# Decoder of twelve sublayers: row-max placements of the short attentions move to the ScalarE queue, and the wide-head attention becomes one Block

## The chip, the core and the metric

One core of a Trainium2 chip runs the whole kernel in one launch. The metric is the device time in microseconds (us); the kernel before took 1625.39 us in the median of 3 runs (1624.26 to 1627.04). The engines are TensorE (PE; its weight loads are listed as PEld), VectorE (DVE), ScalarE (ACT), GpSimd (POOL) and SyncE (SP). SP computes nothing here: it only waits and issues transfers.

## The reference, cut to what matters

A decoder of four layers, each of self-attention, cross-attention and feed-forward, every one with a norm and a residual. x is 8 x 256 x 128 and ctx 8 x 512 x 128, in f32.

```python
x = x + _L0_attn_ref(_layernorm(x, axis=-1), ...)       # linear attention
x = x + _L0_xattn_ref(_layernorm(x, axis=-1), ctx_1024, ...)   # 16 heads of 8, 512 keys
x = x + _L0_ffn_ref(_layernorm(x, axis=-1), ...)        # experts
x = x + _L1_attn_ref(_layernorm(x, axis=-1), ...)       # attention over the batch
x = x + _L1_xattn_ref(_layernorm(x, axis=-1), ctx_1024, ...)   # ONE head of 128, 512 keys
x = x + _L1_ffn_ref(_layernorm(x, axis=-1), ...)
x = x + _L2_attn_ref(_layernorm(x, axis=-1), ...)
x = x + _L2_xattn_ref(_layernorm(x, axis=-1), ctx_1024, ...)   # 16 heads of 8, 512 keys
x = x + _L2_ffn_ref(_layernorm(x, axis=-1), ...)
x = x + _L3_attn_ref(_layernorm(x, axis=-1), ...)       # 16 heads of 8, 256 keys, causal
x = x + _L3_xattn_ref(_layernorm(x, axis=-1), ctx_1024, ...)   # the same with a key mask
x = x + _L3_ffn_ref(_layernorm(x, axis=-1), ...)
```

Each attention is softmax(q k^T / sqrt(d)) v, with the row maximum taken off before the exponential.

## The kernel before

The stages follow each other in `decoder`. A stage is one `Block`: in it each engine runs a program of its own, ordered against the others by semaphores, and at its end all engines meet. The activations lie transposed in SBUF, features on the partitions: xT (128 x 2048) and its norm xn.

**The narrow attentions** (16 heads of 8) are `narrow_attention` = `project` + `attend_wide` (512 keys, in layers 0 and 2) or `attend_short` (256 keys, causal: layer 3's self-attention, then its cross-attention). `project` makes q and k and splits each into three bf16 parts. SP stores the parts to DRAM scratch with `store_parts` (L744) and reads them back with `load_stacks` (L1004) as stacks: `q_stack[par]` and `k_stack[par]` hold, for a pair of heads, 48 rows of part products, a mask row, and in q_stack two rows for the negated row maximum, split into two bf16 parts. There are two stacks of each, by the parity of the batch, and a stack is loaded in two halves of four head pairs.

The attention runs in steps s = 0 to 8, and step s works on two batches at once: in front, the scores of batch s, from which DVE takes the row maxima (L1544); behind, the logits, exponentials and sums of batch b = s - 1. Step 0 has only a front, step 8 only a back. A step goes through i = 0 to 15, one head each. In `attend_short` PE does for each i: with i even a mask matmul for the scores (L1405), then in `logit_bank` a wait until the exponential of head i - 2 is done (there are two logit banks), then the scores (L1422, L1424) and logits (L1444, L1446) of head i; at odd i a piece of the sums with v (L1459, L1461), which waits until POOL has masked the diagonals (L1132) of the group's four exponentials. ACT does the 16 exponentials of a step (L1521, 128 x 384).

A row maximum reaches the stack in this way, once per half hf of the 16 heads: DVE (L1553), POOL splits it into two parts (L1104, L1106), PE transposes it (`turn_max`, L1155; at i = 11 for half 0 of batch s, at i = 3 of the next step for half 1), ACT copies it to `max_rows` (`keep_max`, L1169), and SP issues two transfers of it into `q_stack` (`place`, L1063). PE waits for that placement, and for the loads of the stack, in `attend_halves` at i = 0 and i = 8.

SP's order is written out in `attend_transfers`. For 256 keys (`early`) it is: both halves of load(1), place(0,0), wait for all parts, store k of batches 2 and 3, place(0,1), store q of batches 2 to 7, and then for each s: load(s,1), place(s-1,1), a k store at s = 2 and 3, load(s+1,0), place(s,0). load(2, .) waits for the whole q store and the first k store (`stored_q`, `stored_k1`), and for the logits that free the stack. Every placement stands behind what SP issued or waited for before it.

**The wide-head attention** (L1_xattn) comes after `batch_attention` and takes three Blocks: `fetch` (SP loads its weights), `layer_norm` (PE, ACT and DVE), and `wide_head_attention`, in which SP then begins to load ctxT (L2300), POOL copies xn (L2310), and PE projects q (L2328), k (L2332) and v (L2337) of a batch and makes the scores (L2356), again with the back of the batch before beside the front of the next. A norm is a chain over four tiles of 512 columns: mean (PE, L230), centring (DVE, L265), squares (ACT), variance (PE, L207), root (ACT), reciprocal (DVE, L271), spread (PE, L207), scaling (DVE, L280).

Of the kernel before, what the change touches and what calls it, by code (L numbers as in the profile page):

```python
# [323 lines left out]
def norm_dve(norm, dve):  # L324
# [7 lines left out]
    for t in range(4):  # L332
        if t < 2:
            norm.invert(dve, t + 2)
        norm.scale(dve, t)


def layer_norm(c, padded=None):

    norm = Norm(c, Carver(c), padded=padded)
    with c.nc.Block() as block:

        @block.tensor
        def _(pe):
            norm_pe(norm, pe)

        @block.scalar  # L350
        def _(act):
            norm_act(norm, act)

        @block.vector
        def _(dve):
            norm_dve(norm, dve)
    norm.advance()


class FirstLoads:  # L360
# [681 lines left out]
    body(B // 2, 0, False, True, True)  # L1042


def attend_transfers(c, buf, sp, nk, key_mask, made):


    g = c.sig

    def load(b, hf):  # L1050

        if b > 1:

            sp.wait_ge(g["logits"].sem, g["logits"].at((b - 2) * H + H // 2 * (hf + 1)))
            sp.wait_ge(g["stored_q"].sem, g["stored_q"].at(STORES))
            sp.wait_ge(g[f"stored_k{b // 2}"].sem, g[f"stored_k{b // 2}"].at(STORES))
        load_stacks(c, sp, b % 2, hf, b * S, b * nk, nk, b * S if key_mask else None)

    def place(s, hf):

        sp.wait_ge(g["turned_out"].sem, g["turned_out"].at(s * 2 + hf + 1))
        for e in range(2):
            sp.dma_start(c.q_stack[s % 2][64 * e + ROW_MAX:64 * e + ROWS, HALF * hf:HALF * hf + HALF, :],  # L1063
                         buf.maxrow[hf][8 * e:8 * e + 8, :]).then_inc(g[f"max_placed{hf}"].sem, 16)

    for hf in range(2):
        load(1, hf)
    early = nk == S
    if early:
        place(0, 0)  # L1070
    sp.wait_ge(g["parts"].sem, g["parts"].at(made.parts))
    if early:
        store_parts(c, sp, "k", nk, 1, 2, g["stored_k1"].sem)
        place(0, 1)
    store_parts(c, sp, "q", nk, 1, B // 2, g["stored_q"].sem)
    if not early:
        store_parts(c, sp, "k", nk, 1, 2, g["stored_k1"].sem)
        place(0, 0)
        place(0, 1)
    for s in range(1, B + 1):  # L1080
        k = s if early else s + 1
        if s > 1:
            if s < B:
                load(s, 1)
            place(s - 1, 1)
        if 2 <= k < 4:
            store_parts(c, sp, "k", nk, k, k + 1, g[f"stored_k{k}"].sem)
        if s < B - 1:
            load(s + 1, 0)
        if s < B:  # L1090
            place(s, 0)
    for hf in range(2):
        sp.wait_ge(g[f"max_placed{hf}"].sem, g[f"max_placed{hf}"].at(32 * B))

# [287 lines left out]
def attend_short(c, key_mask, made, gated=False):  # L1382
# [115 lines left out]
    def scalar(act):  # L1498

        act.activation(c.small[:, 648:649], c.consts[:, C_EPS:C_EPS + 1], ACT.Exp)  # L1500

        def keep(grp, b):
            act.wait_ge(g["summed"].sem, g["summed"].at(b * GROUPS + grp + 1))
            act.activation(buf.summed[:, grp, bass.ds(b * S, S)], ps[:, 6 + grp % 2, 0:S], ACT.Identity)\
               .then_inc(g[f"summed_out{grp % 2}"].sem, 1)

        def step(it, par, front, back, before):
            first = isinstance(it, int) and it == 0
            s = it * 2 + par
            b = s - 1  # L1510
            for i in range(H):
                if back and i == 3:
                    keep_max(c, buf, act, b, 1, first)
                if front and i == 11:
                    keep_max(c, buf, act, s, 0, first and par == 0)
                if back:
                    act.wait_ge(g["logits"].sem, g["logits"].at(b * H + i + 1))

                    if not (first and i < 8):
                        act.wait_ge(g["summed"].sem, g["summed"].at(b * GROUPS + (i - 8) // 4 + 1))  # L1520
                    act.activation(buf.probs[i % 8][:, 0:3 * P], ps[:, 4 + i % 2, 0:3 * P], ACT.Exp, scale=scale)\  # L1521
                       .then_inc(g["probs"].sem, 1)
                if before and i == 4:
                    keep(3, s - 2)
                if back and i == 12:
                    keep(1, b)
            if not front:
                keep(3, b)
        attend_steps(nc, ENG.Activation, step)
# [730 lines left out]
              spread=2 * NU, residual=NU, out_proj=NU, probs=NU, max_raw=NU, summed=2 * NU, recip=NU)  # L2260


def wide_head_attention(c, slot):


    nc, g, ps = c.nc, c.sig, c.ps
# [8 lines left out]
    pr = [cv.f32(2, SC) for _ in range(2)]  # L2275
    pT = cv.f32(nch, S)
    sm = c.small
    mx, nb, sums, rec = (fold(sm[:, 4 * i:4 * i + 4], (2, 2)) for i in range(4))
    SCALE = D ** -0.5

    def steps(engine, body):
# [7 lines left out]
    with nc.Block() as block:  # L2289

        @block.sync
        def _(sp):
            def body(it):
                for par in range(2):
                    b = it * 2 + par
                    at = b * SC if isinstance(it, int) else sp.snap(b * SC)
                    if not isinstance(it, int):

                        wait_counted(c, sp, g["v_proj"].sem, g["v_proj"].at(b - 1))
                    sp.dma_start(csrc[par][:, :], c.io["ctxT"][:, bass.ds(at, SC)]).then_inc(g[f"src_in{par}"].sem, 16)  # L2300
            pairs(nc, ENG.SP, body)

        @block.gpsimd
        def _(pool):
            def body(it):
                for par in range(2):
                    b = it * 2 + par
                    if not isinstance(it, int):
                        pool.wait_ge(g["v_proj"].sem, g["v_proj"].at(b - 1))
                    pool.tensor_copy(qsrc[par][:, :], c.xn[:, bass.ds(b * S, S)]).then_inc(g["staged"].sem, 1)  # L2310
            pairs(nc, ENG.Pool, body)

        @block.tensor
        def _(pe):
            pe.wait_ge(g[f"loaded{slot}"].sem, g[f"loaded{slot}"].at(16))

            def step(it, par, front, back):
                first = isinstance(it, int) and it == 0 and par == 0
                second = isinstance(it, int) and it == 0 and par == 1
# [2 lines left out]
                if front:  # L2322
# [15 lines left out]
                                       w[:, W_V:W_V + P], start=True, stop=True)  # L2338
                    mm.then_inc(g["v_proj"].sem, 1)
                if back:  # L2340
                    for t in range(2):
                        pe.wait_ge(g["normed"].sem, g["normed"].at(b * 2 + t + 1))
                        if not second:
                            pe.wait_ge(g["turned_out"].sem, g["turned_out"].at((b - 1) * 2 + t + 1))
                        for ch in range(nch):
                            mm = pe.transpose(ps[:, 5 + t, ch * P:(ch + 1) * P], pr[prv][:, t, ch * P:(ch + 1) * P],
                                              c.ident[:, :])
                        mm.then_inc(g["turned"].sem, 1)
# [9 lines left out]
                if back:  # L2358
                    pe.wait_ge(g["turned_out"].sem, g["turned_out"].at(s * 2))
                    if not second:  # L2360
                        pe.wait_ge(g["residual"].sem, g["residual"].at(b))
                    for ch in range(nch):
                        mm = pe.matmul(ps[:, 7, 0:S], v[prv][:, ch, :], pT[:, ch, :], start=(ch == 0), stop=(ch == nch - 1))
                    mm.then_inc(g["summed"].sem, 1)
            steps(ENG.PE, step)

        @block.scalar
        def _(act):
            def step(it, par, front, back):
# [18 lines left out]
                if front:  # L2388
                    for t in range(2):
                        act.wait_ge(g["maxed"].sem, g["maxed"].at(s * 2 + t + 1))  # L2390
                        act.activation(pr[par][:, t, :], ps[:, 3 + t, :], ACT.Exp, bias=nb[:, par, t:t + 1], scale=SCALE,
                                       accum_out=sums[:, par, t:t + 1]).then_inc(g["probs"].sem, 1)
            steps(ENG.Activation, step)

        @block.vector
        def _(dve):
            def step(it, par, front, back):
# [17 lines left out]
                if front:  # L2415
                    for t in range(2):
# [2 lines left out]
                        dve.wait_ge(g["recip"].sem, g["recip"].at(s * 2 + t + 1))  # L2419
                        dve.tensor_scalar(pr[par][:, t, :], pr[par][:, t, :], rec[:, par, t:t + 1], None, ALU.mult)\  # L2420
                           .then_inc(g["normed"].sem, 1)
            steps(ENG.DVE, step)
    g.advance(staged=B, q_proj=B, k_proj=B, v_proj=B, q_kept=B, k_kept=B, v_kept=B, normed=2 * B, turned=2 * B,
              turned_out=2 * B, probs=2 * B, scores=2 * B, residual=B, summed=B, max_raw=2 * B, maxed=2 * B, recip=2 * B,
              src_in0=16 * B // 2, src_in1=16 * B // 2)
# [862 lines left out]
    return Program(sync, tensor, scalar, vector, gpsimd, advance, norm=norm)  # L3288


def fetch(c, slot, name):


    with c.nc.Block() as block:

        @block.sync
        def _(sp):
            load_weights(c, sp, slot, name)


def narrow_attention(c, slot, name, ctx_keys=0, mask=None, key_mask=False, begun=False, gated=False):

    made = project(c, slot, name, ctx_keys or S, bool(ctx_keys), key_mask, begun, gated)
# [81 lines left out]
def decoder(nc, io):  # L3385
    with ExitStack() as ctx:
# [2 lines left out]
        run(c, narrow_attention(c, 0, "w_l0x", ctx_keys=SC, mask="given"))  # L3389
        combine_into(c, 0, experts(c))  # L3390
        batch_attention(c)
        fetch(c, 0, "w_l1x")
        layer_norm(c)
        wide_head_attention(c, 0)
        token_shift_ffn(c)
        shift_attention(c, 1, "w_l2a")
        run(c, narrow_attention(c, 0, "w_l2x", ctx_keys=SC))
# [160 lines left out]
```

## Time and profile before

| what | value |
|---|---|
| median of 3 runs | 1625.39 us (1624.26 to 1627.04) |
| the profiled execution | 1619.48 us, its span 1617.8 us |
| mean granted TensorE clock in it | 0.954 |
| busy: PE / DVE / ACT / POOL | 1439.9 / 992.2 / 804.3 / 455.9 us |
| layer 3's self-attention, steps 0 to 8 | about 1268 to 1385 us of the span |
| layer 3's cross-attention, steps 0 to 8 | about 1430 to 1548 us |
| wide-head attention with its norm | from 728.6 us on |

The span is what the trace covers; the execution's own time is 1.7 us longer. An engine's busy time counts neither its waits nor the issuing of transfers: for SP, the time of the instructions that issue transfers is listed as SPq. "[x <-engine thing]" behind a row is the idle time of that engine before it and what ended the idle time.

### The profile page before, as it was taken

The page shows a single profiled execution, that of the slowest core. Times are in us where ns is not written, and L with a number is a line of the kernel's source. Part 1 is how long each engine was busy: PE and PEld are TensorE (multiplying, and loading weights), DVE is VectorE, ACT ScalarE, POOL GpSimd, SP SyncE. Part 2 cuts the span into 40 slices and gives each one's busy share as a digit, 9 for nine tenths or more (in the row PEclk, how much of TensorE's full clock was granted, in tenths as well). Part 3 has the DMA queues.
Part 4 walks back from the last instruction along what each step waited for, and adds up shares of the span by engine and source line. Part 5 has one row for each costly group of instructions (what it writes and reads, how often), then busy time and mean ns, then how long its engine had stood idle before and what let it go on. Part 6 is the DMA issues. An engine that isn't in the chain of part 4 may idle for free. (4 is left out here: it accounts for less than half of the span.)

```text
span 1617.8 us, 30013 instructions
## 1 busy us (share of the span) xinstructions
PE 1439.9 (89%) x10746; PEld 725.6 (45%) x10746; DVE 992.2 (61%) x1940; ACT 804.3 (50%) x1498; POOL 455.9 (28%) x656
## 2 busy tenths in 40 slices
PE   7998899999999999878987899899977788978887
PEld 5777634444454443536653452222334333433354
DVE  5666488888163221364557759998376667356746
ACT  4455437677633332304541054777754456445647
POOL 7111220000003567240035430000021456134531
PEclk9999999999999999979997899999986989898999
DMA  2000263221110000001000055322000431143100
GB/s 102 1 0 0 98 203 100 54 51 30 52 69 1 1 0 0 1 1 46 18 7 1 0 161 169 100 54 50 20 13 9 167 100 50 37 167 101 51 2 27
DMA packets 82393, 85.45 MB, mean 53 GB/s; under 512 B 7244, under 2 KB 67916, under 8 KB 81772
## 3 DMA queue, kind: packets, MB, share of 16 engines
q1 hardware_dynamic: 82296, 84.18, 16.9%
q8 instruction: 57, 0.93, 0.2%
q14 instruction: 40, 0.33, 0.1%
HBM read 51.06 MB, written 32.51 MB: 52 GB/s over the span
## 5 line engine op out<-in xcount | busy, mean ns | idle before, releaser
L1335 ACT ACTIVATE arena<-ps 128x1024 f32<-128x1024 f32 x256 | 261.8, 1023 | 109.4 <-PE ps L1242 108.9
L1227 PE MATMUL ps<-k_stack,q_stack 49*128 49x512 bf16 x512 | 190.6, 382 | 14.5 <-DVE small L1358 12.1
L1242 PE MATMUL ps<-q_stack,k_stack 51*128 51x256 bf16 x1024 | 189.6, 272 | 0.6 <-ACT arena L1335 0.4
L1355 DVE CUSTOM_DVE_ANT_0 small<-ps,mask_b 128x512 bf16<-128x512 f32 x256 | 168.0, 689 | 29.6 <-PE ps L1227 28.1
L1358 DVE TENSOR_REDUCE small<-ps 128x1 f32<-128x512 f32 x256 | 162.0, 685 | 15.9 <-PE ps L1227 14.9
L1544 DVE TENSOR_REDUCE small<-ps 128x6 f32<-128x768 f32 x128 | 122.6, 958 | 76.3 <-PE ps L1424 73.8
L1254 PE MATMUL ps<-arena,v_pad 128*32 128x256 f32 x2048 | 162.4, 391 | 1.1 <-ACT arena L1335 1.1
L1521 ACT ACTIVATE arena<-ps 128x384 f32<-128x384 f32 x256 | 118.0, 488 | 78.4 <-PE ps L1446 77.7
L1132 POOL TENSOR_SCALAR_AFFINE_SELECT arena<-arena 128x256 f32<-128x256 f32 x256 | 101.8, 406 | 86.6 <-ACT arena L1521 86.3
L2602 DVE TENSOR_TENSOR arena<-ps,arena 128x512 f32<-128x512 f32 x64 | 44.3, 692 | 101.1 <-PE ps L2519 101.0
L2676 POOL TENSOR_TENSOR arena<-arena 128x512 f32<-128x512 f32 x64 | 79.7, 1266 | 94.3 <-ACT arena L2571 94.3
L1104 POOL TENSOR_TENSOR small<-small 128x16 bf16<-128x16 f32 x64 | 13.8, 216 | 310.8 <-DVE small L1361 281.5
L1234 PE MATMUL ps<-mask_b,ident_b 64*128 64x512 bf16 x512 | 99.9, 383 | 0.5
L1227 PEld LDWEIGHTS ps<-k_stack,q_stack 49*128 49x128 bf16 x512 | 47.6, 93 | 110.9 <-DVE small L1358 80.9
L1242 PEld LDWEIGHTS ps<-q_stack,k_stack 51*128 51x128 bf16 x1024 | 75.2, 95 | 29.0 <-issue 6.8
L2565 ACT ACTIVATE arena<-ps 128x512 f32<-128x512 f32 x64 | 38.2, 597 | 90.1 <-PE ps L2515 90.1
L984 POOL TENSOR_TENSOR arena<-arena 128x512 bf16<-128x512 f32 x40 | 45.5, 1158 | 111.5 <-ACT arena L887 111.5
L2544 PE MATMUL ps<-arena 128*128 128x512 f32 x128 | 66.1, 602 | 0.7
L2515 PE MATMUL ps<-xn,arena 128*128 128x512 f32 x128 | 66.5, 601 | 0.0
L2519 PE MATMUL ps<-xn,arena 128*128 128x512 f32 x128 | 66.3, 600 | 0.0
L1254 PEld LDWEIGHTS ps<-arena,v_pad 128*32 128x32 f32 x2048 | 41.0, 108 | 55.5 <-issue 52.5
L1405 PE MATMUL ps<-mask_b,ident_b 128*128 128x256 bf16 x256 | 52.2, 287 | 14.9 <-DMA q_stack<-max_rows 14.7
(357 smaller groups left out, 2983.7 us busy)
## 6 DMA issues: line engine op xcount, KB each, us to landing
q_stack<-q_scratch SPq DMA_DIRECT2D x128, 96.0 KB
k_stack<-k_scratch SPq DMA_DIRECT2D x64, 192.0 KB
k_scratch<-arena SPq DMA_DIRECT2D x8, 768.0 KB, 3.9
k_stack<-k_scratch SPq DMA_DIRECT2D x64, 96.0 KB
q_scratch<-arena SPq DMA_DIRECT2D x4, 1152.0 KB, 7.5
arena<-in_ctxT SPq DMA_DIRECT2D x8, 512.0 KB, 6.3
k_scratch<-arena SPq DMA_DIRECT2D x8, 512.0 KB, 4.7
k_scratch<-arena SPq DMA_DIRECT2D x16, 256.0 KB, 3.8
```

The source lines that it names most:

```text
L1132: pool.affine_select(diag, diag, [[0, 2], [1, P]], ALU.is_ge, 0.0, 0, -1).then_inc(g["masked"].sem, 1)
L1227: pe.matmul(ps[:, t, :], c.q_stack[par][64 * e:64 * e + ROW_MAX, pr, t * P:(t + 1) * P], c.k_stack[par][64 * e:64 * e + ROW_MAX, pr, :], s ...
L1234: return pe.matmul(ps[:, 2 + 2 * (i % 2) + half, :], c.ident_b[r, :], c.mask_b[r, m:m + 2 * S], start=first, stop=False, skip_group_check= ...
L1242: mm = pe.matmul(ps[:, bank, (ch % 2) * S:(ch % 2 + 1) * S], c.k_stack[prv][64 * e:64 * e + ROWS, pr, ch * P:(ch + 1) * P], c.q_stack[prv] ...
L1254: mm = pe.matmul(ps[32 * j:32 * j + 32, 6 + grp % 2, 0:S], c.v_pad[par][:, piece, head_of(i), :], buf.probs[i % 8][:, piece * S:(piece + 1 ...
L1335: act.activation(buf.probs[i % 8], ps[:, bank:bank + 2, :].rearrange("p a n -> p (a n)"), ACT.Exp, scale=scale).then_inc(g["probs"].sem, 1)
L1355: dve.tensor_tensor_reduce(buf.junk[t], ps[:, t, :], c.mask_b[:, M_X + t * SC:M_X + (t + 1) * SC], 1.0, FLOOR, op0=ALU.add, op1=ALU.max, a ...
L1358: dve.tensor_reduce(out, ps[:, t, :], X, ALU.max).then_inc(g["maxed"].sem, 1)
L1521: act.activation(buf.probs[i % 8][:, 0:3 * P], ps[:, 4 + i % 2, 0:3 * P], ACT.Exp, scale=scale)\
L1544: dve.tensor_reduce(buf.m3[par][:, hf, :, pr % HALF, :], ps[:, bank:bank + 2, 0:3 * P].rearrange("p e (a n) -> p e a n", a=3), X, ALU.max)\
L2515: pe.matmul(ps[:, 2 + u % 2, :], w13[:, (ex * 4 + j) * P:(ex * 4 + j + 1) * P], x, start=True, stop=True)\
L2676: pool.tensor_tensor(slot(v), slot(v), share_e[v // 2 % 2], ALU.mult).then_inc(g["act_made"].sem, 1)
```

## The change

1. `place` becomes the function `place_max`, called with the engine that issues it. In `attend_short` ACT calls it right behind `keep_max` (i = 3 and i = 11). In `attend_wide` SP keeps it.
2. `attend_transfers` is written anew. All narrow attentions: load(1), wait for the parts, store k of batches 2 and 3, store q, then for s = 0 to 8: load(s,1), [SP's placement of half 1], a k store at s = 1 and 2, load(s+1,0), [SP's placement of half 0]. For 512 keys that is the old order but for the first two stores, which swap places. For 256 keys the placements are gone from SP, and each k store comes one s earlier.
3. The wide-head attention is one Block: the weights' load, the norm and the attention. Its norm has arena tiles and PSUM banks of its own (mean and spread in banks 4 to 7, variance in 2 and 3), and the small tiles of the attention move. SP issues weights and ctxT at the start; POOL's first copies wait for scaled tiles of the norm.

```diff
+def place_max(c, buf, eng, s, hf, par):
+    g = c.sig
+    eng.wait_ge(g["turned_out"].sem, g["turned_out"].at(s * 2 + hf + 1))
+    for e in range(2):
+        eng.dma_start(c.q_stack[par][64 * e + ROW_MAX:64 * e + ROWS, HALF * hf:HALF * hf + HALF, :],
+                      buf.maxrow[hf][8 * e:8 * e + 8, :]).then_inc(g[f"max_placed{hf}"].sem, 16)
...
+    by_sp = nk > S
     for hf in range(2):
         load(1, hf)
-    early = nk == S
-    if early:
-        place(0, 0)
     sp.wait_ge(g["parts"].sem, g["parts"].at(made.parts))
-    if early:
-        store_parts(c, sp, "k", nk, 1, 2, g["stored_k1"].sem)
-        place(0, 1)
+    store_parts(c, sp, "k", nk, 1, 2, g["stored_k1"].sem)
     store_parts(c, sp, "q", nk, 1, B // 2, g["stored_q"].sem)
-    if not early:
-        store_parts(c, sp, "k", nk, 1, 2, g["stored_k1"].sem)
-        place(0, 0)
-        place(0, 1)
-    for s in range(1, B + 1):
-        k = s if early else s + 1
-        if s > 1:
-            if s < B:
-                load(s, 1)
-            place(s - 1, 1)
-        if 2 <= k < 4:
-            store_parts(c, sp, "k", nk, k, k + 1, g[f"stored_k{k}"].sem)
-        if s < B - 1:
+    for s in range(B + 1):
+        if 2 <= s < B:
+            load(s, 1)
+        if s and by_sp:
+            place_max(c, buf, sp, s - 1, 1, (s - 1) % 2)
+        if s in (1, 2):
+            store_parts(c, sp, "k", nk, s + 1, s + 2, g[f"stored_k{s + 1}"].sem)
+        if 1 <= s < B - 1:
             load(s + 1, 0)
-        if s < B:
-            place(s, 0)
+        if s < B and by_sp:
+            place_max(c, buf, sp, s, 0, s % 2)
...
                 if back and i == 3:
                     keep_max(c, buf, act, b, 1, first)
+                    place_max(c, buf, act, b, 1, 1 - par)
                 if front and i == 11:
                     keep_max(c, buf, act, s, 0, first and par == 0)
+                    place_max(c, buf, act, s, 0, par)
...
+    norm = Norm(c, cv, mean=(4, 5, 6, 7), var=(2, 3, 2, 3), spread=(4, 5, 6, 7))
...
+            load_weights(c, sp, slot, name)
             pairs(nc, ENG.SP, body)
...
+                    if isinstance(it, int):
+                        pool.wait_ge(g["ln_scaled"].sem, g["ln_scaled"].at(3 * par + 1))
...
+            norm_pe(norm, pe)
+            pe.wait_ge(g[f"loaded{slot}"].sem, g[f"loaded{slot}"].at(16))
             steps(ENG.PE, step)
...
         batch_attention(c)
-        fetch(c, 0, "w_l1x")
-        layer_norm(c)
-        wide_head_attention(c, 0)
+        wide_head_attention(c, 0, "w_l1x")
```

In the wide-head Block ACT and DVE get `norm_act` and `norm_dve` ahead of their steps in the same way.

## Rows read from the trace of the kernel before

**Rows 1.** The page, its head and section 1: busy us, share, instructions.
```profile
span 1617.8 us, 30013 instructions
PE 1439.9 (89%) x10746; PEld 725.6 (45%) x10746; DVE 992.2 (61%) x1940; ACT 804.3 (50%) x1498; POOL 455.9 (28%) x656
```

**Rows 2.** Timeline, norm and first batch of the wide-head attention: start, us, engine, line, form.
```profile
728.59 0.33 SPq L721 DMA_DIRECT2D att_w<-in_w_l1x  x1
729.37 3.67 PE L230 MATMUL ps<-xT,mean_w 128*128 128x512 f32 x8 [1.77 <-PEq L3294]
...
738.15 2.03 PE L207 MATMUL ps<-ident,small 128*128 128x128 f32 x16
741.17 7.53 SPq L2300 DMA_DIRECT2D arena<-in_ctxT  x3
744.07 1.12 PE L2328 MATMUL ps<-arena,att_w 128*128 128x256 f32 x2 [3.89 <-DMA arena<-in_ctxT]
748.00 1.88 PE L2356 MATMUL ps<-arena 128*128 128x512 f32 x4
749.72 0.59 PE L2328 MATMUL ps<-arena,att_w 128*128 128x256 f32 x2
...
751.01 1.05 PE L2337 MATMUL ps<-att_w,arena 128*128 128x128 f32 x8
```

**Rows 3.** Windows, the wide-head attention's start: us, busy by engine, clock, DMA share, GB/s.
```profile
742.00:748.00 6.00, 3.93 (x12) 2.75 (x13) 0.00 (x0) 1.52 (x3) 0.00 (x0) 0.72 0.27 87
```

**Rows 4.** Timeline of SP, layer 3's self-attention, steps 0 to 2.
```profile
1272.35 0.44 SPq L1004 DMA_DIRECT2D k_stack<-k_scratch  x1
1274.83 1.30 SPq L1063 DMA_DIRECT2D q_stack<-max_rows  x2
...
1279.70 1.28 SPq L1063 DMA_DIRECT2D q_stack<-max_rows  x2
1281.02 2.02 SPq L744 DMA_DIRECT2D q_scratch<-arena  x3
1290.15 0.33 SPq L1004 DMA_DIRECT2D q_stack<-q_scratch  x1
...
1291.98 1.27 SPq L1063 DMA_DIRECT2D q_stack<-max_rows  x2
```

**Rows 5.** Timeline of PE, step 2 of layer 3's self-attention, then of its cross-attention.
```profile
1294.49 0.61 PE L1405 MATMUL ps<-mask_b,ident_b 128*128 128x256 bf16 x2 [6.16 <-DMA q_stack<-max_rows]
...
1306.28 0.27 PE L1155 MATMUL ps<-ident_b,small 128*16 128x128 bf16 x2 [0.75 <-POOL small L1106]
...
1457.91 0.61 PE L1405 MATMUL ps<-mask_b,ident_b 128*128 128x256 bf16 x2 [7.29 <-DMA q_stack<-max_rows]
```

**Rows 6.** The line view of L1405, both short attentions: releaser, idle us in total, times.
```profile
  DMA q_stack<-max_rows: 14.7, 4
```

**Rows 7.** Windows, step 2 of layer 3's self-attention behind its stall.
```profile
1294.50:1306.70 12.20, 11.45 (x104) 4.07 (x104) 5.87 (x10) 5.53 (x14) 5.12 (x14) 0.61 0.41 130
```

**Rows 8.** Timelines of PE, ACT and POOL, an undisturbed step of the same attention.
```profile
1335.15 0.39 PE L1405 MATMUL ps<-mask_b,ident_b 128*128 128x256 bf16 x2
...
1338.15 0.37 ACT L1169 ACTIVATE max_rows<-ps 16x256 bf16<-16x256 bf16 x1 [0.26 <-PE ps L1155]
1338.45 0.49 ACT L1521 ACTIVATE arena<-ps 128x384 f32<-128x384 f32 x1
1339.01 0.41 POOL L1132 TENSOR_SCALAR_AFFINE_SELECT arena<-arena 128x256 f32<-128x256 f32 x1 [0.65 <-ACT arena L1521]
1339.74 0.64 PE L1459 MATMUL ps<-arena,v_pad 128*32 128x256 f32 x8 [0.24 <-issue]
...
1344.17 0.27 PE L1155 MATMUL ps<-ident_b,small 128*16 128x128 bf16 x2 [0.52 <-POOL small L1106]
```

**Rows 9.** The line views of L1063 and L721: ns min/median/max of one issue.
```profile
L1063 SPq DMA_DIRECT2D q_stack<-max_rows x128: 610/617/787, 226.9 to 1539.8; - x128
L721 SPq DMA_DIRECT2D att_w<-in_w_l1x x1: 328/328/328, 728.6 to 728.6; - x1
```

More of the change, by code:

```diff
@@ L335, in norm_dve @@
         norm.scale(dve, t)
[L338 to L357, printed above, removed]
 class FirstLoads:
@@ L1057, in load @@
         load_stacks(c, sp, b % 2, hf, b * S, b * nk, nk, b * S if key_mask else None)
[L1059 to L1064, printed above, removed]
+    by_sp = nk > S
     for hf in range(2):
         load(1, hf)
-    early = nk == S
-    if early:
-        place(0, 0)
     sp.wait_ge(g["parts"].sem, g["parts"].at(made.parts))
-    if early:
-        store_parts(c, sp, "k", nk, 1, 2, g["stored_k1"].sem)
-        place(0, 1)
+    store_parts(c, sp, "k", nk, 1, 2, g["stored_k1"].sem)
     store_parts(c, sp, "q", nk, 1, B // 2, g["stored_q"].sem)
-    if not early:
-        store_parts(c, sp, "k", nk, 1, 2, g["stored_k1"].sem)
-        place(0, 0)
-        place(0, 1)
-    for s in range(1, B + 1):
-        k = s if early else s + 1
-        if s > 1:
-            if s < B:
-                load(s, 1)
-            place(s - 1, 1)
-        if 2 <= k < 4:
-            store_parts(c, sp, "k", nk, k, k + 1, g[f"stored_k{k}"].sem)
-        if s < B - 1:
+    for s in range(B + 1):
[6 more added lines that the diff above has]
+        if 1 <= s < B - 1:
             load(s + 1, 0)
-        if s < B:
-            place(s, 0)
+        if s < B and by_sp:
+            place_max(c, buf, sp, s, 0, s % 2)
     for hf in range(2):
@@ L2260, in batch_attention, with wide_head_attention @@
               spread=2 * NU, residual=NU, out_proj=NU, probs=NU, max_raw=NU, summed=2 * NU, recip=NU)
-def wide_head_attention(c, slot):
+def wide_head_attention(c, slot, name):
     nc, g, ps = c.nc, c.sig, c.ps
@@ L2277, in wide_head_attention @@
     sm = c.small
-    mx, nb, sums, rec = (fold(sm[:, 4 * i:4 * i + 4], (2, 2)) for i in range(4))
+    mx, nb, sums, rec = (fold(sm[:, 32 + 4 * i:36 + 4 * i], (2, 2)) for i in range(4))
+    norm = Norm(c, cv, mean=(4, 5, 6, 7), var=(2, 3, 2, 3), spread=(4, 5, 6, 7))
     SCALE = D ** -0.5
@@ L2314, in _ @@
         def _(pe):
-            pe.wait_ge(g[f"loaded{slot}"].sem, g[f"loaded{slot}"].at(16))
             def step(it, par, front, back):
@@ L2340, in step @@
                 if back:
+                    if second:
+                        pe.wait_ge(g["ln_scaled"].sem, g["ln_scaled"].at(4))
                     for t in range(2):
@@ L2392, in step @@
                                        accum_out=sums[:, par, t:t + 1]).then_inc(g["probs"].sem, 1)
+            norm_act(norm, act)
+            act.wait_ge(g[f"loaded{slot}"].sem, g[f"loaded{slot}"].at(16))
             steps(ENG.Activation, step)
@@ L2421, in step @@
                            .then_inc(g["normed"].sem, 1)
+            norm_dve(norm, dve)
+            dve.wait_ge(g[f"loaded{slot}"].sem, g[f"loaded{slot}"].at(16))
             steps(ENG.DVE, step)
+    norm.advance()
     g.advance(staged=B, q_proj=B, k_proj=B, v_proj=B, q_kept=B, k_kept=B, v_kept=B, normed=2 * B, turned=2 * B,
@@ L3288, in lora_ffn @@
     return Program(sync, tensor, scalar, vector, gpsimd, advance, norm=norm)
[L3291 to L3298, printed above, removed]
 def narrow_attention(c, slot, name, ctx_keys=0, mask=None, key_mask=False, begun=False, gated=False):
```

## Prediction, made before the changed kernel was run

> **What bounds the kernel now.** I read the page's busy times first: PE is busy 89% of the span and every other engine 61% or less [rows 1], so a change pays where it takes a wait off PE, and costs where it adds one. Then I looked for the waits of PE in the three places that the change touches. In the wide-head attention, the timeline shows PE finishing the norm at 738.15 + 2.03 = 740.18, and its first projection only at 744.07, released by the ctxT transfer that SP issues at 741.17, when the norm's Block is over [rows 2]. Behind that gap the clock is down: 0.72 on average [rows 3]. In the short attentions the line view of PE's mask matmul shows 14.7 us of waits for the placement of row maxima, in 4 places [rows 6]; two of them are 6.16 and 7.29 us, at the start of step 2 of each attention [rows 5], which leaves 1.25 us for the two others (at i = 8 of step 1, where place(0,1) lands). The SP queue says why [rows 4]: place(1,0) is issued at 1291.98, behind load(2,0) at 1290.15, and that load waited for the q store issued at 1281.02, 9.1 us before. Behind the stall step 2 runs at a clock of 0.61 [rows 7].
>
> **Part 1, the wide-head attention.** (a) Two Block ends go. The weights' issue begins at 728.59, PE's first mean matmul at 729.37 [rows 2]; in one Block both begin together: 0.75 us less. (b) The norm itself keeps its chain. (c) ctxT and weights are issued at the start and have over 10 us to land; in the trace ctxT takes 2.9 us from issue to PE's start (741.17 to 744.07). POOL's first copy waits only for the first scaled tile, its second for all four, and its product is needed by batch 1, 4 us later. So q of batch 0 starts at 740.18, and the clock has no gap to fall in. From the first q matmul to the first scores it now takes 748.00 - 744.07 = 3.93 us, partly at the low level. At the full one, the next batch shows q at 749.72 and v ending at 751.01 + 1.05 less the pipeline's tail, some 2.2 us, with ACT's copy of k beside v. Scores then start at 742.4 instead of 748.00: 5.6 us. Together 6.3 us less. What is late next is the maximum of the first scores on DVE, which follows them as before. Bounds: 4.6 (the idle 3.89 alone and (a)) and 7.
>
> **Part 2, the stall at step 2.** SP was through with load(1) at 1272.35 + 0.44 = 1272.8, then stood until 1274.83 for place(0,0) and until 1279.70 for place(0,1) before the q store [rows 4]. Now the first k store follows at 1272.8 and q at about 1274.3, 6.7 us earlier, so `stored_q` should come near 1284 rather than 1290. The k store of batches 4 and 5, moved ahead of load(2,0), adds some 1.5 us of SP before it, while SP would be waiting anyway, and its bytes stand ahead of the load's on the DMA engines: an estimate of 2 us. load(2,0) also needs the logits of step 1's first half, now later (part 3). It should have landed by 1290, and place(1,0) no longer stands behind it. PE comes to step 2 at 1294.49 - 6.16 = 1288.33 now, and about 2 us later with part 3, so the stall goes. With it goes the low clock: from the first mask to the second turn of maxima the step took 1306.28 - 1294.49 = 11.79 us [rows 5], an undisturbed one 1344.17 - 1335.15 = 9.02 [rows 8], 2.8 us less. Saved: 6.16 + 2.8 = 8.9 in the self-attention, 7.29 + 2.8 = 10.1 in the cross-attention (for the latter I take the same 2.8): 19.0 us. Bounds: 0, if the store stays late, and 19.
>
> **Part 3, what ACT pays.** No transfer is issued by ACT in this trace, so its price must be bounded. On SP one such issue holds the queue 0.617 us in the median and never under 0.610 [rows 9], two take 1.27 [rows 4]. The shortest issue of another kind is 0.33 (one weight tile, [rows 9]). From below I cannot exclude zero: an issue might not hold ACT at all. I take 0.617, because it is the row of the very same transfer, and its minimum shows that it isn't queueing on SP that makes it long.
> What does holding ACT cost? Follow an undisturbed step [rows 8]. keep_max runs 1338.15 to 1338.52, the exponential of head 3 starts at 1338.45, overlapped with it. Now ACT must see its own copy finished (0.03 is what SP needed), issue for 1.27, and then start the exponential (0.04 more) at 1339.86: 1.41 us later. Behind this exponential stand the 12 others of the step, POOL's mask of head 3 (1339.01 to 1339.42) and, on PE, the logits of head 5, which wait for its bank, and the sums of the first group, which start at 1339.74 when POOL is done. They move to 1341.12: 1.38 us on the PE path. PE does nothing else meanwhile, since its program is in order, and nothing later gives it back: its two waits per step for the maxima (0.5 us each, such as the 0.52 at 1344.17) hang on scores that PE itself makes later too. The same holds at i = 11. That is two halves in each of steps 1 to 7 and one in step 8: 15 per attention (the one in step 0 falls where ACT has nothing to do), 30 x 1.38 = 41.4 us. Off this come the 1.25 us at i = 8 of step 1, where the later PE finds place(0,1) landed. Net 40.2. Bounds: 0 and 42.
> The Trainium skill speaks to this twice. Its page DMA: Bandwidth & Descriptors, section Issuing engines are not separate DMA queues, says that spreading transfers over engines saves only the sequencer's time to start them, usually small against the transfer. On SP's row it isn't small: 1.27 us for two transfers of 4 KB. Its page Perfetto Trace Analysis, section DMA Instruction — HWDGE, says that the profiled time of an issue is time in which the sequencer is not free for its next instruction, which speaks against this change; by the first rule part 3 would be near nothing, by the second it is the whole 40.
>
> **Part 4, the rest.** In the wide attentions only the first q and k store swap; their placements stay on SP in the same order, and load(2,0) waits for both stores as before, so I cost it at nothing. What hides it is step 0, which has only scores: ACT needs `stored_q` first at i = 5 of step 1. If that cover were gone, ACT would wait for the k store too, at most the 9 us that the q store took above, twice. The earlier k stores of the short attentions lie under steps 1 and 2.
>
> **The sum.** -6.3 - 19.0 + 40.2 = +14.9 us on a span of 1617.8: 1632.7, and 1634.4 for the execution (1619.48 now). The median of the runs, 1625.39, is 5.9 above the profiled execution; with the same distance the forecast is 1640.3 us, 0.9% slower.
>
> **Rivals.** *ACT is not held.* The issue goes out beside the exponentials, and only parts 1 and 2 count: -25.3 us, 1600. For it: the compute on ACT and the issue of a transfer need different hardware. Against it: SP's rows are spaced by their own durations. It turns the result below the point of break-even: 25.3 + 1.25 over 30 halves is 0.89 us a half, 0.8 us for both issues. 12%.
> *The issue is shorter on ACT.* At 0.33 and 0.44 for the two, the short issues of SP's load rows [rows 4], a half costs 0.77 + 0.11 = 0.88, thirty 26.4, and all comes to about 0: 1625. Against it: the minimum of 0.610. 13%.
> *The clock falls too.* PE now stands about 1.4 us twice in 15 us, beside the 0.5 us waits. The trace shows the clock down after idle stretches of 3.9 and 6.2 us [rows 2, 3, 5, 7] and up in the undisturbed steps; between lies no row. If a third of the 14 full steps ran like the one at 0.61 (2.8 us more), that is +13: 1653. 12%.
> *The stall stays* because the earlier k store delays load(2,0): 19 us not saved, 1659. Speaks against it: 6.7 us of head start against some 2 us of bytes. 5%.
> The forecast's own case has 58%.
>
> **Numbers.** A difference of 0.2% (3.3 us) is about what can be told from no change here. Faster: the first rival and a third of the second, 16%. Same: most of the rest of the second, 8%. Slower: the forecast, the clock and the stall, 76%. The range 1616 to 1655 leaves out the first rival and the upper part of the last two.
>
> **What would show each step.** ACT should have rows that issue q_stack<-max_rows, of about 0.6 us, and its first exponential behind each should start some 1.4 us after keep_max's end; the sums of i = 5 and i = 13 should show PE waiting about 1.4 us more; an undisturbed step should be 2.8 us longer. Step 2 should begin without a wait for max_rows and at full clock. The first q projection should follow the norm's last matmul at once. The prediction is wrong if ACT's exponentials follow the issue in under 0.8 us, or if undisturbed steps stay within 1 us of their length now.

## The result and the profile after

The changed kernel takes 1700.49 us in the median of 4 runs (1692.72 to 1706.09), against 1624.83 us before in the same runs: ratio 1.046, interval 1.0409 to 1.0512. It is slower by about 75 us, where 15 were forecast and 1655 us was the end of the range. The profiled execution took 1692.72 us.

The head of the page after, its row of the granted clock in 40 slices, and the row of the new queue:

```profile
span 1690.9 us, 30018 instructions
PE 1501.9 (89%) x10746; PEld 738.3 (44%) x10746; DVE 992.5 (59%) x1940; ACT 802.7 (47%) x1498; POOL 455.3 (27%) x656
...
PEclk9999999999999999799978999999687776967788
...
q10 hardware_dynamic: 640, 0.26, 0.1%
```

The last row is a queue that the kernel before does not have: 640 packets of ACT's placements. PE is "busy" 62 us more than in [rows 1], with the same 10746 matmuls; DVE, ACT and POOL are busy as before. That is the first sign: the same matmuls take longer. The clock row shows where, in slices 31 to 38, which hold the two short attentions.

**The wide-head attention**, timeline of PE, SP and ACT, to be read against [rows 2]:

```profile
729.80 0.33 SPq L699 DMA_DIRECT2D att_w<-in_w_l1x  x1
729.86 3.67 PE L230 MATMUL ps<-xT,mean_w 128*128 128x512 f32 x8 [1.05 <-PEq L2029]
730.18 17.31 SPq L2276 DMA_DIRECT2D arena<-in_ctxT  x4
...
738.64 2.03 PE L207 MATMUL ps<-ident,small 128*128 128x128 f32 x16
740.51 0.60 PE L2306 MATMUL ps<-arena,att_w 128*128 128x256 f32 x2
740.95 1.02 PE L2310 MATMUL ps<-arena,att_w 128*128 128x512 f32 x2
...
742.84 1.96 PE L2337 MATMUL ps<-arena 128*128 128x512 f32 x4
```

Weights and mean matmul begin together, and q follows the norm with no gap, at the full clock's 0.60 us instead of 1.12. The first scores start at 742.84, 2.3 us after q's start, where the sum had 2.2. This part came as predicted.

**The placements**, line view of L1029 (min/median/max ns of an issue), then ACT in a step of layer 3's self-attention:

```profile
L1029 SPq DMA_DIRECT2D q_stack<-max_rows x64: 610/616/796, 227.6 to 1146.3; - x64
L1029 ACTq DMA_DIRECT2D q_stack<-max_rows x64: 620/621/1266, 1271.9 to 1605.9; - x64
```

```profile
1315.33 0.37 ACT L1142 ACTIVATE max_rows<-ps 16x256 bf16<-16x256 bf16 x1 [0.26 <-PE ps L1128]
1315.73 1.27 ACTq L1029 DMA_DIRECT2D q_stack<-max_rows  x2
1317.18 0.87 ACT L1496 ACTIVATE arena<-ps 128x384 f32<-128x384 f32 x2 [1.48 <-PE ps L1419]
```

An issue on ACT takes what it takes on SP, and the exponential comes only behind both. The idle time of 1.48 us is put down to PE, but PE's logits were long there: it is the issue. On PE the same step shows both waits that the prediction named:

```profile
1315.02 0.27 PE L1128 MATMUL ps<-ident_b,small 128*16 128x128 bf16 x2 [0.48 <-DVE arena L1509]
1317.72 0.23 PE L1395 MATMUL ps<-k_stack,q_stack 49*128 49x128 bf16 x1 [1.21 <-ACT arena L1496]
1318.47 0.64 PE L1432 MATMUL ps<-arena,v_pad 128*32 128x256 f32 x8 [0.41 <-POOL arena L1105]
```

From ACT's copy of the maxima to PE's sums it is 3.14 us here (1315.33 to 1318.47), and 1.59 in [rows 8] (1338.15 to 1339.74): 1.55 more per half.

**The stall** is gone from step 2, but step 1 of the self-attention now has one, since place(0,0) lands late. Line view of PE's mask matmul (releaser, idle us, times), then step 1 of the self-attention in the timelines of ACT and PE:

```profile
  DMA q_stack<-max_rows: 6.1, 2
```

```profile
1271.87 2.04 ACTq L1029 DMA_DIRECT2D q_stack<-max_rows  x2
...
1278.48 0.59 PE L1378 MATMUL ps<-mask_b,ident_b 128*128 128x256 bf16 x2 [4.72 <-DMA q_stack<-max_rows]
```

Of the 14.7 us of [rows 6] 6.1 are left, 4.72 of them at a place that had next to none. In the kernel before, PE waited there for 0.59 us:

```profile
1277.31 0.38 PE L1405 MATMUL ps<-mask_b,ident_b 128*128 128x256 bf16 x2 [0.59 <-DMA q_stack<-max_rows]
```

The other 1.36 us stand at step 1 of the cross-attention. There ACT issues place(0,0) before SP comes to its stores (at 1471.90), and PE goes on 1.96 us after the issue's end; in the self-attention, behind the stores, it took 4.57:

```profile
1471.60 1.29 ACTq L1029 DMA_DIRECT2D q_stack<-max_rows  x2
...
1474.85 0.38 PE L1378 MATMUL ps<-mask_b,ident_b 128*128 128x256 bf16 x2 [1.36 <-DMA q_stack<-max_rows]
```

### The profile page after: what moved, and what is told of

It reads as the page before. It is cut to its first block and busy times, and to the rows that moved or that the text cites. A ratio compares the mean times of both kernels' runs of the same rounds, so it can differ in the third digit from the quotient of the medians.

```text
span 1690.9 us, 30018 instructions
## 1 busy us (share of the span) xinstructions
PE 1501.9 (89%) x10746; PEld 738.3 (44%) x10746; DVE 992.5 (59%) x1940; ACT 802.7 (47%) x1498; POOL 455.3 (27%) x656
## 5 line engine op out<-in xcount | busy, mean ns | idle before, releaser
L1200 PE MATMUL ps<-k_stack,q_stack 49*128 49x512 bf16 x512 | 190.5, 382 | 14.5 <-DVE small L1331 12.2
L1215 PE MATMUL ps<-q_stack,k_stack 51*128 51x256 bf16 x1024 | 189.6, 272 | 0.5 <-ACT arena L1308 0.4
L1227 PE MATMUL ps<-arena,v_pad 128*32 128x256 f32 x2048 | 162.3, 391 | 1.1 <-ACT arena L1308 1.1
L1395 PE MATMUL ps<-k_stack,q_stack 49*128 49x128 bf16 x256 | 61.6, 256 | 33.9 <-ACT arena L1496 33.8
L1417 PE MATMUL ps<-q_stack,k_stack 51*128 51x256 bf16 x256 | 79.8, 346 | 2.1 <-ACT arena L1496 2.0
L1397 PE MATMUL ps<-k_stack,q_stack 49*128 49x256 bf16 x256 | 76.9, 336 | 0.0
L1378 PE MATMUL ps<-mask_b,ident_b 128*128 128x256 bf16 x256 | 64.7, 346 | 6.3 <-DMA q_stack<-max_rows 6.1
L1432 PE MATMUL ps<-arena,v_pad 128*32 128x256 f32 x512 | 60.5, 559 | 9.0 <-POOL arena L1105 8.0
```

The source lines that it names most:

```text
L1200: pe.matmul(ps[:, t, :], c.q_stack[par][64 * e:64 * e + ROW_MAX, pr, t * P:(t + 1) * P], c.k_stack[par][64 * e:64 * e + ROW_MAX, pr, :], s ...
L1215: mm = pe.matmul(ps[:, bank, (ch % 2) * S:(ch % 2 + 1) * S], c.k_stack[prv][64 * e:64 * e + ROWS, pr, ch * P:(ch + 1) * P], c.q_stack[prv] ...
L1227: mm = pe.matmul(ps[32 * j:32 * j + 32, 6 + grp % 2, 0:S], c.v_pad[par][:, piece, head_of(i), :], buf.probs[i % 8][:, piece * S:(piece + 1 ...
L1417: pe.matmul(ps[:, bank, 0:S], k[:, 0:P], q, start=True, stop=True, skip_group_check=True)
```

## The experiments

I measured each trace by one row of PE, the turn of maxima (`turn_max`), which comes once per half of a batch: the time from one turn to the next in the self-attention, averaged over the ten intervals from the turn of batch 2's half 0 to that of batch 7's. These intervals hold no wait for a placement. Times are medians, with their ratio to the kernel before as it ran beside them.

| kernel | us | ratio (interval) | us per half | clock there |
|---|---|---|---|---|
| before | 1624.8 | 1 | 6.33 | 1.00 |
| changed | 1700.5 | 1.046 (1.0409 to 1.0512) | 9.04 | 0.73 |
| e1: wide-head part alone | 1620.0 | 0.9958 (0.9936 to 0.9981) | 6.34 | 1.00 |
| e3: SP's old order, ACT places | 1697.5 | 1.0457 (1.0406 to 1.0508) | 9.42 | 0.66 |
| e4: SP's new order, SP places | 1619.9 | 0.9973 (0.9944 to 1.0001) | 6.33 | 1.00 |
| e5b: changed, filler on PE | 1662.3 | 1.0235 (1.0173 to 1.0297) | 7.95 | 1.00 |
| e6: ACT held by 5 activations | 1693.6 | 1.0426 (1.0363 to 1.0489) | 8.69 | 0.74 |
| e6c: ACT held by 2 | 1652.6 | 1.0174 (1.0113 to 1.0235) | 7.45 | 0.91 |
| e8: one transfer at a time | 1658.3 | 1.0201 (1.014 to 1.0262) | 7.57 | 0.95 |
| e7: SP places, q store split | 1607.1 | 0.9898 (0.9862 to 0.9934) | | |
| e7b: the same, stores first | 1612.2 | 0.9927 (0.9902 to 0.9951) | | |

### e1: the wide-head part alone

The changed kernel with `attend_transfers` and the placements of before.

> Only the wide-head part of the change; the short and wide attentions are as before. In the changed kernel's trace the first projection of the wide-head attention follows the norm without a gap, so this part alone should give about 6 us: 1618 to 1620. If the loss of the changed kernel came from this Block (its instructions or its clock), the time would be well above 1625 instead.

Measured 0.9958, 5 to 7 us. The Block is not the loss; it is a gain of the predicted size.

### e3 and e4: who places, and in which order

e3 lets ACT place, and keeps SP's times by letting SP wait where it placed. e4 is the changed kernel with one line different:

```diff
-    by_sp = nk > S
+    by_sp = True
```
(and without ACT's two calls of `place_max`).

> The changed kernel, but SP stands at each place where it issued a placement before, for the same copy of ACT, and issues none, so loads and stores keep their old times; ACT issues the placements. Theory A (ACT held for two issues per half is the loss): as slow as the changed kernel, 1690 to 1715, since 30 halves are still held. Theory B (the loss comes from SP's new order, stores ahead of what is needed sooner): near 1620 to 1640.

> The changed kernel with SP's new order, but SP issues all placements, as it does for 512 keys. Theory A: no half is held, undisturbed steps are back at some 12.7 us; step 1 waits for place(0,0), which now stands behind the q store (some 5 us and a low clock behind it), step 2 doesn't wait: 1605 to 1625. Theory B: as slow as the changed kernel, about 1690.

With ACT placing, the old order is as slow as the new one; with SP placing, the new order costs nothing. So the whole loss hangs on ACT. e3 also shows that the stall at step 2 goes without the new order: its q store is issued as late as before, and PE waits 1.80 and 1.68 us for placements at step 1 of the two attentions and not at all at step 2, where the held ACT also brings PE later. But e4 also shows that the new order gains nothing over e1 (0.9973 against 0.9958). Its waits for placements, line view and timeline of PE:

```profile
  DMA q_stack<-max_rows: 12.2, 3
```

```profile
1280.21 0.38 PE L1378 MATMUL ps<-mask_b,ident_b 128*128 128x256 bf16 x2 [4.14 <-DMA q_stack<-max_rows]
...
1440.90 0.58 PE L1378 MATMUL ps<-mask_b,ident_b 128*128 128x256 bf16 x2 [7.58 <-DMA q_stack<-max_rows]
```

Both stand at step 1: the stall has moved to the step before, behind the stores that were moved ahead of place(0,0).

### e5b: work for PE while ACT is held

```diff
+                if back and front and i in (5, 13):
+                    for _ in range(FILL):      # FILL = 20
+                        pe.matmul(ps[:, 1, 3 * P:4 * P], c.ident_b[:, :], c.mask_b[:, 0:P], start=True, stop=True,
+                                  skip_group_check=True)
                 if back:
                     logit_bank(i, b, first)
```

> The changed kernel with 20 mask matmuls of 128 columns on PE, into the free columns of bank 1, just ahead of the wait of head 5 and head 13 for their logit bank: PE has work in the time in which ACT is held, and they add nothing that PE would not have waited for anyway. Theory A1 (the larger part of the loss is the clock, which falls behind each idle stretch): the clock in the short attentions is near 1.0 and the time near my forecast, 1635 to 1655. Theory A2 (the held ACT alone, whatever the clock): 1690 to 1715, as the changed kernel or a little above it.

The filler runs in steps 1 to 7. Windows over the ten intervals, the changed kernel first, then e5b (length, busy us of PE, PEld, DVE, ACT and POOL with their counts, clock, DMA share, GB/s):

```profile
1307.18:1397.62 90.44, 74.29 (x743) 25.97 (x741) 45.88 (x80) 40.72 (x100) 37.27 (x105) 0.73 0.15 42
```

```profile
1306.39:1385.87 79.48, 68.30 (x940) 32.73 (x941) 45.67 (x80) 41.39 (x101) 36.96 (x105) 1.00 0.16 47
```

And e5b's PE at one half; compare the 6.33 us from 1337.84 to 1344.17 of the kernel before (the later one is in [rows 8]):

```profile
1330.46 0.27 PE L1128 MATMUL ps<-ident_b,small 128*16 128x128 bf16 x2 [0.81 <-DVE arena L1513]
...
1331.89 1.29 PE L1455 MATMUL ps<-mask_b,ident_b 128*128 128x128 bf16 x20
1333.27 0.23 PE L1395 MATMUL ps<-k_stack,q_stack 49*128 49x128 bf16 x1
...
1338.47 0.27 PE L1128 MATMUL ps<-ident_b,small 128*16 128x128 bf16 x2 [0.52 <-POOL small L1079]
```

Two hundred matmuls more, and the same ten halves take 11 us less, because the clock stays at its upper level. Against the changed kernel the ratio falls from 1.046 to 1.0235: the clock was 2.25% or about 37 us of the loss. The rest, 1.0235 against 0.9958 or about 45 us, stays at full clock; that is the time held. By the intervals of the ratios each of the two is good to some 12 us. The windows say nearly the same by another way: ten halves lose 10.96 us by the clock, thirty 33. The filler fills just the wait: the logits follow it at 1333.27, 0.06 us after the exponential's end. The expectation of 1635 to 1655 was missed by 7 us: a held half costs 1.62 us and not 1.38, see part 3 below.

### e6 and e6c: ACT held without a transfer

e1 (SP places, in the old order) with, behind ACT's copy, a chain of 5 or of 2 one-column activations that each wait for the one before:

```diff
+    act.wait_ge(g["turned_out"].sem, g["turned_out"].at(s * 2 + hf + 1))
+    for k in range(HOLD):
+        act.activation(c.small[:, 656:657], c.consts[:, 0:1], ACT.Identity).then_inc(g["held"].sem, 1)
+        act.wait_ge(g["held"].sem, g["held"].at((s * 2 + hf) * HOLD + k + 1))
```

> SP issues all placements in the order of before and the wide-head part is kept; ACT, instead of issuing, waits for its own copy and then runs a chain of 5 activations of one column, each waiting for the one before (an estimate of 0.25 us a link, 1.25 us in all). Theory A (a held ACT is the loss, whatever holds it): as slow as the changed kernel plus the stall at step 2 that it lost, 1690 to 1720. Theory C (it is the transfer on a second queue, the placements landing late or contention): near 1620.

> The same with a chain of 2, some 0.5 us. Theory A1 (two parts, the time held and, past some length, the clock): 30 halves of 0.5 us are 15 us and the clock stays up, 1630 to 1640. Theory A2 (loss in proportion to the time held, 2.5 us for each half of 1.4 as in the changed kernel): 30 x 0.9 = 27, 1645 to 1655.

ACT in e6, then in e6c:

```profile
1335.87 0.37 ACT L1166 ACTIVATE max_rows<-ps 16x256 bf16<-16x256 bf16 x1 [0.24 <-PE ps L1152]
1336.28 1.14 ACT L1038 ACTIVATE small<-consts 128x1 f32<-128x1 f32 x5
1337.58 0.87 ACT L1520 ACTIVATE arena<-ps 128x384 f32<-128x384 f32 x2 [0.16 <-ACT small L1038]
```

```profile
1344.19 0.37 ACT L1166 ACTIVATE max_rows<-ps 16x256 bf16<-16x256 bf16 x1 [0.31 <-PE ps L1152]
1344.59 0.44 ACT L1038 ACTIVATE small<-consts 128x1 f32<-128x1 f32 x2
1345.20 0.87 ACT L1520 ACTIVATE arena<-ps 128x384 f32<-128x384 f32 x2 [0.17 <-ACT small L1038]
```

With no transfer on ACT and a hold of nearly the same length, the kernel is as slow (1.0426) and the clock as low (0.74). So it is the held engine, and nothing of a second queue. e6c says how the price grows. Its hold puts the exponential 0.7 us later than in the kernel before (1.01 us behind the copy's start instead of 0.30). Seven of its ten intervals run at full clock and take 6.89 to 7.27 us, 0.7 to 0.8 more than the same ones of the kernel before (6.14 to 6.54). The three others take 7.96 to 8.78 us at a clock of 0.64 to 0.80. The kernel is 28 us slower than before, 1652.6, where I had put 1630 to 1640 for two separate parts and 1645 to 1655 for a loss in proportion. The first theory missed by both of its terms: a hold of 0.75 us over 30 halves is 22 us and not 15, and the clock did not stay up. The proportional value fits only by number: the intervals show two kinds, not one stretched kind.

### e8: one transfer at a time

The second of the two issues goes one head later, behind the next exponential.

```diff
+                    place_max(c, buf, act, b, 1, 1 - par, (0,))
+                if back and i == 4:
+                    place_max(c, buf, act, b, 1, 1 - par, (1,))
```
(and likewise at i = 11 and 12).

> The changed kernel, but ACT issues the second transfer of a half one head later, behind the next exponential. The first exponential is 0.75 us late, the second 1.4 us, for which PE, one head further on, has some 0.7 us of slack. Theory A1: each half costs about 0.75 us of PE and leaves it idle for less at a time, the clock stays mostly up: 1620 to 1650. Theory A2 (each issue costs its full time on the path): 1690 to 1710.

```profile
1339.09 0.37 ACT L1142 ACTIVATE max_rows<-ps 16x256 bf16<-16x256 bf16 x1 [0.61 <-PE ps L1128]
1339.49 0.62 ACTq L1029 DMA_DIRECT2D q_stack<-max_rows  x1
1340.28 0.49 ACT L1500 ACTIVATE arena<-ps 128x384 f32<-128x384 f32 x1 [0.82 <-PE ps L1419]
1340.31 0.62 ACTq L1029 DMA_DIRECT2D q_stack<-max_rows  x1
1341.12 0.49 ACT L1500 ACTIVATE arena<-ps 128x384 f32<-128x384 f32 x1 [0.34 <-issue]
```

The second issue runs under the first exponential, at 1340.31, and PE has slack for what is left of it. Eight of the ten intervals run at full clock and take 7.08 to 7.78 us, 0.86 to 1.24 more than the same ones of the kernel before; the two others take 8.69 and 8.73 at a clock of 0.80. This gives back over half of the loss, but ends 8 us above the range I gave: a half costs 0.97 us in the mean and not 0.75, which is 7 us over thirty, and some halves still fall to the low clock.

### e7 and e7b: nothing on ACT, a smaller store to wait for

e1, and in the short attentions the q store in two parts, load(2, .) and load(3, .) waiting for the first. The edit against e1, cut to the order of the stores for 256 keys:

```diff
         store_parts(c, sp, "k", nk, 1, 2, g["stored_k1"].sem)
+        store_parts(c, sp, "q", nk, 1, 2, g["stored_q1"].sem)
         place(0, 1)
-    store_parts(c, sp, "q", nk, 1, B // 2, g["stored_q"].sem)
+        store_parts(c, sp, "q", nk, 2, B // 2, g["stored_q2"].sem)
```

e7b places batch 0's half 0 only behind the first k store and the first q part.

> The wide-head part of the change, SP issuing all placements in the order of before, but in the short attentions the q store is split: batches 2 and 3 right behind the first k store, ahead of place(0,1), the other four batches behind it; load(2, .) and load(3, .) wait for the first part alone. ACT is never held. Theory (the stall at step 2 comes from the size of the store that load(2,0) waits for): the stall of 6 to 7 us at step 2 and the low clock behind it go in both attentions, and place(0,0) still lands in time: some 15 to 19 us below the wide-head part alone, 1601 to 1606. Rival (whatever goes ahead only moves the wait, as in the changed kernel, where the stall went from step 2 to step 1): 1616 to 1621.

> The same with place(0,0) behind the first k store and the first part of the q store. If a placement is late because of the bytes that stand ahead of it (1.6 MB here, 3.1 MB of stores in the changed kernel, nothing but loads in the variant above), step 1 waits some 2 us for it in each attention, with no low clock: 1604 to 1611. If bytes ahead don't matter: the same as the variant above.

The SP queue of e7 and PE's waits for placements in its self-attention:

```profile
1273.46 1.78 SPq L722 DMA_DIRECT2D q_scratch<-arena  x3
1275.51 1.28 SPq L1056 DMA_DIRECT2D q_stack<-max_rows  x2
1276.83 2.00 SPq L722 DMA_DIRECT2D q_scratch<-arena  x3
1278.95 1.15 SPq L982 DMA_DIRECT2D q_stack<-q_scratch  x1
```

```profile
1273.12 0.38 PE L1400 MATMUL ps<-mask_b,ident_b 128*128 128x256 bf16 x2 [0.62 <-DMA q_stack<-max_rows]
...
1286.03 0.39 PE L1400 MATMUL ps<-mask_b,ident_b 128*128 128x256 bf16 x2 [1.89 <-DMA q_stack<-max_rows]
...
1287.53 0.61 PE L1400 MATMUL ps<-mask_b,ident_b 128*128 128x256 bf16 x2
```

The window of step 2 behind that wait, in the columns of the windows above:

```profile
1287.50:1294.02 6.52, 6.52 (x60) 2.27 (x57) 3.08 (x5) 3.38 (x9) 2.88 (x8) 0.51 0.41 138
```

load(2,0) starts 5.5 us after the part that it needs, instead of 9.1 after the whole; it now follows SP's own issue of the second part without a gap. Step 2 waits only 1.89 us, but the clock falls all the same: the first mask pair still takes 0.39 us, the second one 0.61 (as in [rows 5]), and the 6.52 us from 1287.50 on run at a clock of 0.51. e7 is the fastest kernel here: 1607.06 us, 0.9898 of before (0.9862 to 0.9934), some 10 us below e1, so the split gives 0.6% and the rest of the 1% is e1's. I had put 15 to 19, or 1601 to 1606, with no low clock behind step 2. Waits of 1.89 and 1.80 us stay at step 2 of the two attentions, each with 6.5 us of low clock behind it. e7b is 5 us slower in the median, which is the expected direction and size (its 1612.17 lies 1 us above the range), but the two intervals overlap, so I count it as a hint only; its trace does show place(0,0) late in the cross-attention, 3.93 us with a low clock behind it, against 0.94 in e7. In the self-attention it waits 1.17 us against 0.62.

## Why the prediction was wrong

The direction and the mechanism of part 3 (an issue holds ACT, and PE waits behind it) were right. Of 75 us I had 15. Most of the 60 us between them is the clock (37 us), which the sum put at nothing; the hold was 7 us too small, and the stalls gave back some 4 us where parts 2 and 3 had 20 (an estimate: e5b lies 38 us above the kernel before, of which -7 are part 1 and 49 the hold). By the prediction's own steps:

**Part 1** (-6.3 us) held: 0.9958, or 7 us by the ratio.

**Part 3, the price of a half** (1.38 us), was too small in one term. I let the exponential start 0.04 us after the issues; the trace has 0.18 (1315.73 + 1.27 = 1317.00, exponential at 1317.18). From the copy to the sums it is 1.55 us instead of 1.38, and 7.95 - 6.33 = 1.62 per interval at full clock (e5b). Thirty of them are 48.6 us, not 41.4; the last 0.07 us of a half I have not followed. The rival of an issue that costs ACT less is dead, with 0.621 us on ACT against 0.616 on SP. Here the Trainium skill (Perfetto Trace Analysis, section DMA Instruction — HWDGE) was the right page to follow: the issuing sequencer isn't free while an issue lasts, and the trace agrees: ACT's exponential starts 0.18 us behind the 1.27 us of issues.

The 1.25 us taken off in part 3 were misread. I put the two small waits of [rows 6] at i = 8 of step 1, for place(0,1). They stand at i = 0 of step 1, for place(0,0): 0.59 us at 1277.31 and 0.66 at 1439.60. PE was not going to be late there, since nothing is held before it, and it is this very placement that the new order made late.

**The clock** is the term that failed most. I had it as a rival at 12% and +13 us, "a third of the steps"; it was 37 us, and no rival matter: the ten intervals ran at 0.73 on average. The prediction took the idle stretches of 3.9 and 6.2 us as the only rows that tell of a falling clock, and noted that no row lay between. But the undisturbed step already has waits of 0.5 us at the turns, and the hold put 1.2 us more of waiting closely behind each of them, twice a step; e5b shows that filling these 1.2 us is enough to keep the clock up. What the change did to the clock should have been a term of the sum, bounded by a whole attention at the clock of [rows 7]: 28 full halves at 2.8 us for two are 39 us. That this is close to what came is in part luck, since the 2.8 us belong to a clock of 0.61 and the changed kernel ran at 0.73.

**Part 2, the stall at step 2** (-19.0 us) went where it was said to go, but not out of the kernel. The sum left out place(0,0). I argued only for load(2,0), that its store comes earlier, and did not ask what the stores, now issued from 1267.94 on in the changed kernel, stand in front of: 3.1 MB of them ahead of this placement and 0.8 MB issued beside it. The placement was issued by 1273.91, and PE could go on at 1278.48, 4.6 us later; in [rows 4, 5] that was 1.2 us (1291.98 + 1.27 to 1294.49), and in the cross-attention of the changed kernel, where the stores come behind the placement, 2.0. Its own queue on ACT did not let it past. The cause, bytes ahead of it, is argued from these rows; e7b, which varies it, gives only a hint. The Trainium skill says that all issuing engines' transfers interleave on the same 16 DMA engines (DMA: Bandwidth & Descriptors, section Issuing engines are not separate DMA queues), and the three rows fit that. I used the section for part 3 alone and should have used it for part 2. e4 against e1 shows the net of the new order: nothing, 0.9973 against 0.9958. The waits for placements are 12.2 us in e4 and 6.1 in the changed kernel. The difference is the cross-attention, where SP's placement in e4 stands behind SP's own stores (7.58 us) and ACT's is issued before them (1.36). The saving of the low clock behind step 2 was not safe either: e7 has it after a wait of only 1.89 us.

**Part 4** (nothing for the wide attentions) is not contradicted: e4 holds their swapped stores and is no slower than e1 beyond the intervals.

Added up from the ratios against before: -7 (e1) + 45 (held, e5b against e1, the changed stalls in it) + 37 (clock, changed against e5b) = 75. This sum closes by its making, since each term is the step from one kernel to the next; what supports it are the rows, 1.62 us of hold and 1.1 us of clock per half, or 49 and 33 us over thirty.

## What to carry to other kernels

An engine that computes on the critical path is a poor place to issue transfers: count 0.6 us for each against the slack of what stands behind it, and if it must be, issue them one at a time under running work. When an edit puts idle stretches on TensorE, price the clock as a part of the sum and not as a risk, even where no stretch is longer than 1.5 us; an experiment that fills the wait with dummy matmuls tells the two apart. And when a store is moved ahead, ask what small transfer now stands behind its bytes: splitting the store so that the first load waits for its own part gave 0.6% (e7 against e1) where moving the whole gave nothing (e4 against e1).

## What the runs showed of the hardware

- Issuing the same 4 KB transfer costs 0.621 us on ACT and 0.616 on SP; behind it ACT's next activation starts 0.18 us later, about the same as behind a chain of small activations that wait for each other (0.16).
- TensorE can lose its upper clock without a long idle stretch. With waits of about 1.2 and 0.5 us at each half of a step, none longer than 1.5 where [rows 2] have 3.9, the granted clock over ten halves was 0.73 on average, a mix of the levels of 1.2 and 2.4 GHz; with the same waits filled, it stayed at 2.4 (1.00). In e7 one wait of 1.89 us among smaller ones was followed, 1.5 us later, by 6.52 us at 0.51, which is the lower level.
- A small transfer on a queue of its own was not quick while another queue had megabytes in flight: 4.6 us from the end of its issue to PE's start, with 3.1 MB of stores issued ahead of it, against 2.0 in the same kernel with the stores behind it.
